# Router products in halves, product and sum as separate steps, last tile by column halves, in the tail of an attention and feed-forward kernel

## The chip, the cores and the metric

One core of a Trainium2 chip runs the whole layer in one launch. The metric is the device time of that core in microseconds (us); lower is better. The kernel before took 857.85 us, the median of three runs (856.19, 857.85 and 858.23).

## What is computed

```python
# x: (8, 128, 512); 32 heads of width 128; E = 8 routing experts
x = x + xattn(_layernorm(x), ctx, mask, ...)       # cross attention, with its own residual inside
xf = _layernorm(x).reshape(-1, 512)
routing = softmax(xf @ gate_w.T)                   # (1024, 8)
in_scale = routing @ in_channel_scale              # (1024, 512)
out_scale = routing @ out_channel_scale            # (1024, 512)
out = xf * in_scale @ sign(weight).T * out_scale + bias
x = x + out                                        # float32 throughout
```

The change touches the last part alone, the feed-forward with its router, which is done for eight tiles of 128 tokens by 512 channels.

## The kernel before, in words

The order of all work is written out by hand. `schedule()` (L84 and on) returns one list of steps such as `("M", 3, 1)`, and each engine walks the same list and picks the steps it has a function for, in that order (the `walk` calls at the end of each engine's block). Nothing is reordered later: if an engine waits in one step, all its later steps wait too. Engines signal each other by semaphores.

Most of the time goes into projections and attention. Float32 products are made of three products of rounded parts (high by high, high by low, low by high: `three`, L1268 to L1273). The stretch that matters here is the tail, the last 52 us. Its steps are, for a tile `i` of 8 or a pair `p` of 4 (pair `p` holds tiles `2p` and `2p+1`):

- `OUT`: the last attention output products; DVE (VectorE) adds them to `acc`. `ST`, `LN2`, `ROOT`, `LS`: statistics of the layer norm.
- `NT`, `BI`: the normalised tile (ACT, the ScalarE, or DVE for tiles 4 and 6), and the bias added to `acc` by POOL (GpSimd), L758.
- `TX`: the tile transposed on PE (TensorE) and copied by ACT.
- `G`: the router's logits for a pair, 8 products with 8 columns (L1390; the trace shows 16 matmuls), all written to the bank `t`; then the maxima on DVE (L1194) and the exponentials on ACT (L940).
- `ROUTE`: the division on DVE (L1202, L1205, L1209). `RT`, `RTC`: the routing weights transposed on PE (L1399) and copied by ACT (L949).
- `R`: the input scales of a pair, four 256-column products (L1410). `Y`: DVE multiplies them into the tiles (L1221, twice). `YL`: ACT makes the high part (L958, twice), DVE the low part of the first two channel chunks (L1229), POOL that of the other two (L771).
- `OS`: the output scale of one tile on PE (L1417), always into the one bank `out1`, and ACT's copy of it (L963). The next `OS` has to wait for that copy.
- `M`: the large product of a tile, eight 512-column matmuls in two parts of four (L1428, L1429), into bank `proj0` or `proj1` by turns.
- `MP`: three things of one tile in one step: DVE multiplies the product by the output scale (L1237), POOL adds it to `acc` (L779), SP (SyncE) stores the tile (L696). For the last tile DVE makes the sum itself (L1242).
- `KEEP`: six 512-column matmuls into `s1` that nothing reads (L1439).

The tiles of the product, `res_tiles`, are two buffers, so `MP` of tile `i` waits for POOL's sum of tile `i-2`. The large product of tile `i` waits for DVE's `MP` of tile `i-2`, which frees its bank.

## Time and profile before

| | |
|---|---|
| median of 3 runs | 857.85 us |
| the profiled execution, its own time | 855.55 us |
| its span, first to last instruction | 853.8 us |
| mean granted TensorE clock | 0.996 of full |
| PE, busy share of the span | 98% |
| tail, 800 to 854 us: PE, DVE, ACT, POOL busy | 46.2, 27.7, 24.9, 23.8 us |

The profile is one execution. Times of rows are counted from the start of its span. A busy PE is not PE at its peak: what matters here are the gaps between its matmuls and the clock that was granted. A gap is shown with the instruction that ended it.

### The profile page before, as it was taken

To read this page: it belongs to the slowest core of one execution; us is meant where nothing else is said; L and a number is where in the kernel's file an instruction comes from. 1 tells how busy PE (TensorE), PEld (TensorE's weight loads), DVE (VectorE), ACT (ScalarE), POOL (GpSimd) and SP (SyncE) were. 2 spreads that over 40 slices of the span, in tenths; PEclk is the share of its full clock that TensorE was granted. 3 is DMA by queue.
4 is the path that set the end of the run, shared out by engine and by line. 5 is a ranking of instruction groups with operands and counts; after the bars stand their busy time and mean duration, and the time that the engine had idled before them with its cause. 6 is when DMAs were issued, how large, how long until landed. Compare 5 with 4: busy or idle time off the path is not lost.

```text
span 853.8 us, 12843 instructions
## 1 busy us (share of the span) xinstructions
PE 840.0 (98%) x4354; PEld 703.1 (82%) x4354; DVE 623.4 (73%) x1000; ACT 391.8 (46%) x1007; POOL 302.9 (35%) x280
## 2 busy tenths in 40 slices
PE   9999999999999999999999999999999999999996
PEld 8878888888888877888888888888888888888874
DVE  5787846778776786868777777777777787787654
ACT  5632422432431444544544554454455445446662
POOL 2013211022030043525545544554454345434236
PEclk9999999999999999999999999999999999999999
DMA  8355463673443659414214313421441342150001
GB/s 272 134 178 181 157 226 135 183 256 133 133 166 111 222 190 292 143 53 152 99 59 152 135 53 125 152 104 55 154 141 54 116 152 99 59 210 8 1 25 74
DMA packets 60576, 114.07 MB, mean 134 GB/s; under 512 B 5192, under 2 KB 38600, under 8 KB 55264
## 3 DMA queue, kind: packets, MB, share of 16 engines
q1 hardware_dynamic: 60512, 113.25, 38.9%
q8 instruction: 36, 0.59, 0.3%
q14 instruction: 28, 0.23, 0.1%
HBM read 77.58 MB, written 35.65 MB: 133 GB/s over the span
## 4 chain that ended last, share of the span: by engine, by line
PE 87%; DVE 7%; ACT 2%; issue 2%; DMA 1%; POOL 0%; DVEq 0%; POOLq 0%; ACTq 0%; SPq 0%
PE out L1270 10%; PE out L1272 10%; PE out L1271 10%; PE proj L1270 9%; PE proj L1272 9%; PE proj L1271 9%; PE s L1342 6%; PE o L1361 6%; PE s L1272 3%; PE s L1270 3%; PE s L1271 3%; PE t L1350 3%; PE proj L1428 1%; PE proj L1429 1%; PE s L1318 1%
## 5 line engine op out<-in xcount | busy, mean ns | idle before, releaser
L878 ACT ACTIVATE probs<-probs,neg_max 128x128 f32<-128x128 f32 x256 | 99.7, 391 | 136.5 <-DVE neg_max L1132 136.4
L717 POOL TENSOR_TENSOR w_stage<-w_stage 128x256 f32<-128x256 f32 x30 | 24.5, 817 | 311.5 <-DMA w_stage<-in_wk 149.3
L729 POOL TENSOR_TENSOR w_lo<-w_stage,w_hi 128x512 fp32r<-128x512 f32 (+1 forms) x52 | 59.2, 1148 | 144.3 <-ACT w_hi L816 144.3
L1270 PE MATMUL out<-wo_hi,o_hi 128*128 128x512 f32 x224 | 95.3, 425 | 0.6 <-DVE acc L1166 0.6
L1166 DVE TENSOR_TENSOR acc<-out,acc 128x512 f32<-128x512 f32 x100 | 68.3, 687 | 34.4 <-PE out L1272 33.8
L1270 PE MATMUL proj<-x_hi,w_hi 128*128 128x512 f32 x210 | 88.5, 422 | 0.2 <-DVE ring L991 0.2
L1272 PE MATMUL out<-wo_lo,o_hi 128*128 128x512 f32 x224 | 88.3, 394 | 0.0
L1271 PE MATMUL out<-wo_hi,o_lo 128*128 128x512 f32 x224 | 87.6, 391 | 0.0
L1272 PE MATMUL proj<-x_lo,w_hi 128*128 128x512 f32 x210 | 82.7, 394 | 0.0
L1271 PE MATMUL proj<-x_hi,w_lo 128*128 128x512 f32 x210 | 82.0, 391 | 0.0
L741 POOL TENSOR_TENSOR bias_mask<-bias_raw,mask_neg 128x512 f32<-128x512 f32 x64 | 76.1, 1200 | 11.0 <-DVE probs L1129 10.9
L1139 DVE TENSOR_TENSOR probs<-probs,inv_sum 128x512 f32<-128x512 f32 x64 | 70.1, 1096 | 2.2
L816 ACT ACTIVATE w_hi<-w_stage 128x512 fp32r<-128x512 f32 (+1 forms) x113 | 61.7, 567 | 17.7 <-PE out L1272 3.4
L896 ACT ACTIVATE o_hi<-o 128x512 fp32r<-128x512 f32 x60 | 35.7, 595 | 46.7 <-PE o L1361 46.7
L1146 DVE TENSOR_TENSOR o_lo<-o,o_hi 128x512 fp32r<-128x512 f32 x60 | 41.0, 683 | 20.1 <-ACT o_hi L896 20.0
L1007 DVE TENSOR_TENSOR w_lo<-w_stage,w_hi 128x512 fp32r<-128x512 f32 (+1 forms) x61 | 42.8, 702 | 10.8 <-ACT w_hi L816 10.1
L1272 PEld LDWEIGHTS out<-wo_lo,o_hi 128*128 128x128 f32 x224 | 42.0, 188 | 9.5
L1270 PEld LDWEIGHTS out<-wo_hi,o_hi 128*128 128x128 f32 x224 | 42.3, 189 | 8.0 <-issue 2.1
L878 ACT ACTIVATION_READ_ACCUMULATOR probs<-probs,neg_max 128x1 f32 x256 | 47.9, 187 | 0.0
L1271 PEld LDWEIGHTS out<-wo_hi,o_lo 128*128 128x128 f32 x224 | 42.5, 190 | 6.0
L886 ACT ACTIVATE probs_t<-t 128x512 f32<-128x512 f32 x64 | 37.5, 586 | 21.1 <-PE t L1350 19.7
L1272 PEld LDWEIGHTS proj<-x_lo,w_hi 128*128 128x128 f32 x210 | 39.4, 188 | 9.0
(343 smaller groups left out, 2151.0 us busy)
## 6 DMA issues: line engine op xcount, KB each, us to landing
k_spill<-ring SPq DMA_DIRECT2D x64, 256.0 KB, 2.8
v_spill<-ring SPq DMA_DIRECT2D x64, 256.0 KB, 2.2
w_stage<-in_wk SPq DMA_DIRECT2D x32, 256.0 KB, 3.3
big_stage<-in_wv SPq DMA_DIRECT2D x8, 1024.0 KB, 7.9
w_stage<-in_wq SPq DMA_DIRECT2D x32, 256.0 KB, 4.2
k_first<-k_spill SPq DMA_DIRECT2D x8, 1024.0 KB, 6.6
v_first<-v_spill SPq DMA_DIRECT2D x8, 1024.0 KB, 4.8
wo_raw<-in_wo SPq DMA_DIRECT2D x16, 512.0 KB, 3.3
```

The lines of the kernel that those rows point to most:

```text
L729: pool.tensor_tensor(lo, staged(m, part), hi.bitcast(F32), ALU.subtract).then_inc(g_wlo, 1)
L741: pool.tensor_tensor(bias_mask[:, j % 2], bias_raw[:, i % 2][:, None, :].to_broadcast([P, HALF, P]), mask_neg[:, halves[half], :], ALU.add ...
L816: act.activation(hi, staged(m, part), ACT.Copy).then_inc(a_whi, 1)
L878: last = act.activation(probs[:, j % 2, b, :], probs[:, j % 2, b, :], ACT.Exp, bias=neg_max[:, col:col + 1], accum_out=row_sum[:, col:col ...
L1007: dve.tensor_tensor(lo, staged(m, part), hi.bitcast(F32), ALU.subtract).then_inc(v_wlo, 1)
L1139: dve.tensor_tensor(probs[:, j % 2], probs[:, j % 2], inv_sum[:, cols, None].to_broadcast([P, HALF, P]), ALU.mult).then_inc(v_probs, 1)
L1166: dve.tensor_tensor(acc[:, b, :], bank_tensor[:], acc[:, b, :], ALU.add).then_inc(v_acc, 1)
L1270: pe.matmul(to[:], left_hi, right_hi, start=first and n == 0, stop=False, skip_group_check=True)
L1271: pe.matmul(to[:], left_lo, right_hi, start=False, stop=False, skip_group_check=True)
L1272: last = pe.matmul(to[:], left_hi, right_lo, start=False, stop=n == len(pairs) - 1, skip_group_check=True)
L1342: last = pe.matmul(to[:, b * P:(b + 1) * P], queries[:, b * P:(b + 1) * P], keys, start=True, stop=True)
L1361: last = pe.matmul(to[:, b * P:(b + 1) * P], v_tiles[p % 2][:, half * HALF + b, i * P:(i + 1) * P], probs_t[:, j % 2, b * P:(b + 1) * P], ...
```

## The change

It is confined to the tail's order and to its last two tiles.

- The router's step is split: `GA` (first tile of a pair) and `G` (second tile), each 4 products, with other PE work between them for pairs 1, 2 and 3. DVE's and ACT's part stays at `G`.
- `MP` is split: `MP` is now DVE's product, and the new step `SUM` is the sum and the store. The sum of tile 6 goes from POOL to DVE.
- The last tile's large product is made by column halves: eight 256-column matmuls into `proj1`, then eight into `t`. DVE multiplies and adds each half by itself, and SP stores each by itself.
- `KEEP` is gone. The steps of the tail stand in another order.

```diff
+    def routed(p):
+        return [("RT", p), ("RTC", p)]
-              ("TX", 4), ("TX", 5), ("TX", 6), ("TX", 7), ("MP", 1), ("M", 2, 0), ("G", 2), ("ROUTE", 2), ("BI", 4), ("M", 2, 1), ("OS", 2),
-              ("M", 3, 0), ("RT", 2), ("RTC", 2), ("G", 3), ("R", 2), ("Y", 2), ("M", 3, 1), ("YL", 2), ("MP", 2), ("OS", 3), ("KEEP", 0),
-              ("OS", 4), *large(4), ("ROUTE", 3), ("RT", 3), ("RTC", 3), ("R", 3), ("Y", 3), ("MP", 3), ("BI", 5), ("OS", 5), *large(5),
-              ("YL", 3), ("MP", 4), ("BI", 6), ("OS", 6), *large(6), ("MP", 5), ("BI", 7), ("OS", 7), *large(7), ("MP", 6), ("MP", 7)]
...
+    steps += [("GA", 2), ("M", 2, 0), ("G", 2), ("BI", 4), ("M", 2, 1), ("ROUTE", 2), ("OS", 2), ("M", 3, 0), *routed(2), ("GA", 3),
+              ("R", 2), ("Y", 2), ("M", 3, 1), ("YL", 2), ("G", 3), ("MP", 2), ("SUM", 2), ("OS", 3), ("OS", 4), ("ROUTE", 3), ("BI", 5)]
+    steps += [("M", 4, 0), *routed(3), ("MP", 3), ("M", 4, 1), ("R", 3), ("Y", 3), ("YL", 3), ("SUM", 3), ("OS", 5), *large(5), ("MP", 4), ("BI", 6),
+              ("SUM", 4), ("OS", 6), *large(6), ("MP", 5), ("BI", 7), ("SUM", 5), ("OS", 7), *large(7), ("MP", 6), ("SUM", 6), ("MP", 7), ("SUM", 7)]
...
+                elif i == B - 1:
+                    dve.wait_ge(a_os, B)
+                    dve.wait_ge(g_res, B - 2)
                     dve.wait_ge(g_xb, B)
+                    for part, cols in enumerate(last_columns):
+                        dve.wait_ge(pe_ffn, B + part)
+                        dve.tensor_tensor(res_tiles[:, i % 2, cols], last_bank[part][:, 0:D // 2],
+                                          out_scale_halves[1][:, i % HALF, cols], ALU.mult).then_inc(v_prod, 1)
+                        dve.wait_ge(v_prod, B + part)
+                        dve.tensor_tensor(acc[:, i, cols], acc[:, i, cols], res_tiles[:, i % 2, cols], ALU.add).then_inc(v_last_res, 1)
...
-            def router(p):
-                if p == 0:
+            def router(p, r):
+                if p == 0 and r == 0:
                     pe.wait_ge(d_ffn_small, 80)
-                to = take(t_bank)
-                for i in (2 * p, 2 * p + 1):
-                    pe.wait_ge(a_nt, i + 1)
-                    for c in range(DC):
-                        last = pe.matmul(to[:, i % 2 * E:i % 2 * E + E], nt_pairs[p][:, i % 2, c * P:(c + 1) * P], gate_sb[:, c, :],
-                                         start=c == 0, stop=c == DC - 1)
...
-            def keep_busy(_):
-
-                to = take(s_bank[1])
-                for _ in range(KEEP_BUSY):
-                    last = pe.matmul(to[:], sign_w[:, 0, 0:P], sign_w[:, 0, :], start=True, stop=True)
-                last.then_inc(pe_kept, 1)
+            def last_product(part, toks):
+
+                to = take(last_bank[part])
+                for c in range(DC):
+                    pe.matmul(to[:, 0:D // 2], scaled_hi[:, c, toks], sign_w[:, c, last_columns[part]], start=c == 0, stop=False)
+                    last = pe.matmul(to[:, 0:D // 2], scaled_lo[:, c, toks], sign_w[:, c, last_columns[part]], start=False,
+                                     stop=c == DC - 1)
+                last.then_inc(pe_ffn, 1)
```

PE from the second part of tile 3 to the input scales of pair 3, before (L1417 is `OS`, L1439 `KEEP`, L1428 and L1429 a large product, L1399 `RT`, L1410 `R`):

```order
L1417 MATMUL out<-x_lo,x_hi 128x512
L1439 MATMUL s<-x_hi 128x512 x6
L1417 MATMUL out<-x_lo,x_hi 128x512
...
L1399 MATMUL s<-ident,routing 64x128 x2
L1410 MATMUL o<-x_hi,x_lo 128x256 x2
L1410 MATMUL out<-x_hi,x_lo 128x256 x2
```

and with the change (L1415 is the second half of the router for pair 3, L1449 `OS`, L1463 and L1464 a large product, L1431 `RT`, L1442 `R`):

```order
L1415 MATMUL t<-gate_sb,k_second 128x8 x4
L1449 MATMUL out<-x_lo,x_hi 128x512 x2
L1463 MATMUL proj<-x_hi 128x512
...
L1431 MATMUL s<-ident,routing 64x128 x2
L1463 MATMUL proj<-x_hi 128x512
...
L1442 MATMUL o<-x_hi,x_lo 128x256 x2
```

The six filling matmuls are gone, the router's second half stands directly ahead of two `OS` with nothing between them, and half of tile 4's large product has moved between `RT` and `R`.

DVE from the scaled tiles of pair 3 to its end, before (L1221 `Y`, L1237 `MP`, L1229 the low part of `YL`, L1242 the last sum):

```order
L1221 TENSOR_TENSOR k_second<-out0,k_second 128x512
L1237 TENSOR_TENSOR k_first<-proj1,v_first 128x512
L1229 TENSOR_TENSOR x_lo<-k_second,x_hi 128x2x256
L1237 TENSOR_TENSOR k_first<-proj0,v_second 128x512
L1237 TENSOR_TENSOR k_first<-proj1,v_second 128x512
L1237 TENSOR_TENSOR k_first<-proj0,v_second 128x512
L1237 TENSOR_TENSOR k_first<-proj1,v_second 128x512
L1242 TENSOR_TENSOR acc<-acc,k_first 128x512
```

and with the change (L1250 `MP`, L1232 `Y`, L1240 low part, L1258 the sum of tile 6, L1265 and L1268 product and sum of the last tile's halves):

```order
L1250 TENSOR_TENSOR k_first<-proj1,v_first 128x512
L1232 TENSOR_TENSOR k_second<-o,k_second 128x512
L1232 TENSOR_TENSOR k_second<-out0,k_second 128x512
L1240 TENSOR_TENSOR x_lo<-k_second,x_hi 128x2x256
...
L1250 TENSOR_TENSOR k_first<-proj0,v_second 128x512
L1258 TENSOR_TENSOR acc<-acc,k_first 128x512
L1265 TENSOR_TENSOR k_first<-proj1,v_second 128x256
L1268 TENSOR_TENSOR acc<-acc,k_first 128x256
L1265 TENSOR_TENSOR k_first<-t,v_second 128x256
L1268 TENSOR_TENSOR acc<-acc,k_first 128x256
```

`MP` of tile 3 moved ahead of `Y` of pair 3, and one sum of the old last tile became a sum of tile 6 and four half-width operations.

POOL's last operations, before (L779 a sum, L758 the bias, L771 its half of `YL`):

```order
L771 TENSOR_TENSOR x_lo<-wo_raw,x_hi 128x2x256
L779 TENSOR_TENSOR acc<-acc,k_first 128x512 x2
L758 TENSOR_TENSOR acc<-acc,ffn_bias_bc 128x512
L771 TENSOR_TENSOR x_lo<-k_second,x_hi 128x2x256
L779 TENSOR_TENSOR acc<-acc,k_first 128x512
```

and with the change (L790 a sum, L769 the bias, L782 its half of `YL`):

```order
L782 TENSOR_TENSOR x_lo<-wo_raw,x_hi 128x2x256
L790 TENSOR_TENSOR acc<-acc,k_first 128x512
L769 TENSOR_TENSOR acc<-acc,ffn_bias_bc 128x512
L782 TENSOR_TENSOR x_lo<-k_second,x_hi 128x2x256
L790 TENSOR_TENSOR acc<-acc,k_first 128x512
```

The sum of tile 3 moved from ahead of POOL's half of pair 3 to behind it; behind the rows shown stand a bias, a sum, a bias and a sum in both orders (tiles 6, 5, 7, 6 before; 6, 4, 7, 5 now).

## Rows read from the trace of the kernel before

**Rows 1.** The page: span, PE, and granted clock in 40 slices.
```profile
span 853.8 us, 12843 instructions
...
PEclk9999999999999999999999999999999999999999
```

**Rows 2.** Busy time by stretches (us: length, then each engine, clock, DMA share, GB/s).
```profile
800.00:854.00 54.00, 46.16 (x230) 34.84 (x228) 27.70 (x63) 24.86 (x53) 23.79 (x19) 0.94 0.11 40
```

**Rows 3.** The same view around the two slow stretches.
```profile
812.80:816.30 3.50, 3.50 (x11) 2.66 (x10) 2.69 (x11) 1.89 (x5) 1.40 (x1) 0.53 0.00 0
...
840.20:843.60 3.40, 3.31 (x8) 2.46 (x8) 1.23 (x3) 0.24 (x1) 3.29 (x3) 0.52 0.20 76
```

**Rows 4.** PE in order of time: start, us, what, [idle before, releaser].
```profile
802.15 0.48 PE L1270 MATMUL out<-x_lo,o_hi 128*128 128x512 f32 x1
...
808.17 0.38 PE L1399 MATMUL s<-ident,routing 128*64 128x128 f32 x2 [0.34 <-ACT w_stage L935]
...
810.54 1.95 PE L1390 MATMUL t<-gate_sb,w_stage 128*128 128x8 f32 x16
...
822.66 1.12 PE L1324 MATMUL s<-ident,ring 128*128 128x128 f32 x8 [0.34 <-ACT k_first L935]
...
837.81 0.50 PE L1410 MATMUL o<-x_hi,x_lo 64*128 64x256 f32 x2 [0.47 <-ACT x_hi L949]
838.15 0.39 PE L1410 MATMUL out<-x_hi,x_lo 64*128 64x256 f32 x2
838.38 0.39 PE L1417 MATMUL out<-x_lo,x_hi 64*128 64x512 f32 x1
840.29 0.78 PE L1428 MATMUL proj<-x_hi 128*128 128x512 f32 x1 [1.51 <-DVE k_first L1237]
```

**Rows 5.** The chain that ended last: start, us, what.
```profile
833.07 1.58 PE s L1439 x6
...
843.20 0.43 PE proj L1428
...
848.20 0.23 PE proj L1429
```

**Rows 6.** ACT in order of time.
```profile
831.10 0.27 ACT L940 ACTIVATE exps<-t,logit_neg_max 128x8 f32<-128x8 f32 x1 [1.52 <-DVE logit_neg_max L1194]
...
831.50 0.20 ACT L940 ACTIVATION_READ_ACCUMULATOR exps<-t,logit_neg_max 128x1 f32 x1
...
833.18 0.58 ACT L963 ACTIVATE v_first<-out 128x512 f32<-128x512 f32 x1
...
839.30 1.14 ACT L958 ACTIVATE x_hi<-k_second 128x512 fp32r<-128x512 f32 x2
```

**Rows 7.** DVE in order of time.
```profile
827.47 0.37 DVE L1205 TENSOR_SCALAR routing<-exps,exps_inv 128x16 fp32r<-128x16 f32 x2
...
834.19 1.74 DVE L1205 TENSOR_SCALAR routing<-exps,exps_inv 128x16 fp32r<-128x16 f32 x2
...
849.64 1.54 DVE L1242 TENSOR_TENSOR acc<-acc,k_first 128x512 f32<-128x512 f32 x1
```

**Rows 8.** POOL in order of time.
```profile
833.35 1.30 POOL L771 TENSOR_TENSOR x_lo<-wo_raw,x_hi 128x512 fp32r<-128x512 f32 x1 [7.18 <-ACT x_hi L958]
834.62 1.28 POOL L779 TENSOR_TENSOR acc<-acc,k_first 128x512 f32<-128x512 f32 x1
840.31 1.66 POOL L779 TENSOR_TENSOR acc<-acc,k_first 128x512 f32<-128x512 f32 x1 [4.42 <-DVE k_first L1237]
...
843.16 1.27 POOL L771 TENSOR_TENSOR x_lo<-k_second,x_hi 128x512 fp32r<-128x512 f32 x1
...
849.37 1.26 POOL L779 TENSOR_TENSOR acc<-acc,k_first 128x512 f32<-128x512 f32 x1
```

**Rows 9.** DVE's narrow tensor operation, from the groups by shape.
```profile
L1032 DVE TENSOR_TENSOR w_lo<-w_stage,w_hi 128x256 fp32r<-128x256 f32 x7 | 2.7, 421 | 4.3 <-ACT w_hi L832 4.3
```

**Rows 10.** The stores of the output, by tile: DMA time from issue to landing.
```profile
DMA to landing us min/median/max: 2.0/2.0/3.1
```

More of the change, by code:

```diff
@@ L691, in store @@
             def store(i):
-                if i < B - 1:
+                if i == B - 1:
+                    for part, cols in enumerate(last_columns):
+                        sp.wait_ge(v_last_res, part + 2)
+                        sp.dma_start(out[i][:, cols], acc[:, i, cols]).then_inc(d_out, 16)
+                    return
+                if i == B - 2:
+                    sp.wait_ge(v_last_res, 1)
+                else:
                     sp.wait_ge(g_res, i + 1)
-                else:
-                    sp.wait_ge(v_last_res, 1)
                 sp.dma_start(out[i], acc[:, i, :]).then_inc(d_out, 16)
             walk({"WL": pair_weights, "DL": second_plain_pair, "VL": value_weights, "SAVE": save, "ML": mask_load, "XL": x_load, "KV": keys_and_values,
-                  "BL": bias_load, "WOL": output_weights, "AL": residual_load, "SMALL": small_loads, "FW": ffn_weights, "MP": store})
-            sp.wait_ge(d_out, 16 * B)
+                  "BL": bias_load, "WOL": output_weights, "AL": residual_load, "SMALL": small_loads, "FW": ffn_weights, "SUM": store})
+            sp.wait_ge(d_out, 16 * (B + 1))
         @block.gpsimd
@@ L1381, in ffn_transpose, with first_router, second_router @@
                 read_by(ffn_bank(i), a_nt, i + 1)
-            def router(p):
-                if p == 0:
+            def router(p, r):
+                if p == 0 and r == 0:
                     pe.wait_ge(d_ffn_small, 80)
-                to = take(t_bank)
-                for i in (2 * p, 2 * p + 1):
-                    pe.wait_ge(a_nt, i + 1)
-                    for c in range(DC):
-                        last = pe.matmul(to[:, i % 2 * E:i % 2 * E + E], nt_pairs[p][:, i % 2, c * P:(c + 1) * P], gate_sb[:, c, :],
-                                         start=c == 0, stop=c == DC - 1)
-                last.then_inc(pe_gate, 1)
-                read_by(to, a_rexp, p + 1)
+                to = t_bank if r else take(t_bank)
+                pe.wait_ge(a_nt, 2 * p + r + 1)
+                for c in range(DC):
+                    last = pe.matmul(to[:, r * E:(r + 1) * E], nt_pairs[p][:, r, c * P:(c + 1) * P], gate_sb[:, c, :],
+                                     start=c == 0, stop=c == DC - 1)
+                if r:
+                    last.then_inc(pe_gate, 1)
+                    read_by(to, a_rexp, p + 1)
+            def first_router(p):
+                router(p, 0)
+            def second_router(p):
+                router(p, 1)
             def transpose_routing(p):
@@ L1433, in ffn_product @@
                     read_by(to, v_prod, i + 1)
[L1435 to L1440 removed]
+            def last_product(part, toks):
+                to = take(last_bank[part])
+                for c in range(DC):
+                    pe.matmul(to[:, 0:D // 2], scaled_hi[:, c, toks], sign_w[:, c, last_columns[part]], start=c == 0, stop=False)
+                    last = pe.matmul(to[:, 0:D // 2], scaled_lo[:, c, toks], sign_w[:, c, last_columns[part]], start=False,
+                                     stop=c == DC - 1)
+                last.then_inc(pe_ffn, 1)
             walk({"WARM": warm_up, "D": plain_product, "P": product, "X": transpose_x, "S": score, "T": transpose_probs,
[L1443 to L1444 removed]
+                  "PV": probs_times_values, "OUT": output, "TX": ffn_transpose, "GA": first_router, "G": second_router, "RT": transpose_routing,
+                  "R": routed_scales, "OS": routed_out_scale, "M": ffn_product})
 def kernel(**inputs):
```

37 lines of the change are left out of this document (22 added, 15 removed).

## The prediction, on record before the run

> **What bounds the kernel now.** I read the page first. PE is the busiest engine, and its clock is full in every one of the 40 slices [rows 1]. The change leaves everything up to about 802 us alone, so I read the tail by stretches: there the mean granted clock is 0.94 and PE is busy 46.2 of 54 us [rows 2]. At most some 8 us are thus in question. Smaller windows show the clock at 0.53 from 812.8 to 816.3 and at 0.52 from 840.2 to 843.6 [rows 3], which is its lower level, 1.2 GHz, nearly throughout. I call each a fall. The chain prices it: a large matmul takes 0.43 us at the low level and 0.23 at the full one [rows 5], so the eight in such a stretch lose 8 x 0.20 = 1.6 us. What PE did before each fall: 16 router matmuls with 8 columns in 1.95 us before the first; short products and waits of 0.47 and 1.51 us before the second [rows 4].
>
> PE's order of time shows its waits: 0.34 (`RT`, pair 0), 0.34 (`TX`), 0.47 (`R`, pair 3), 1.51 (large product of tile 5, behind DVE's `MP` of tile 3) [rows 4]. The chain shows the six filling matmuls in a row, 1.58 us [rows 5].
>
> The end is not PE's alone. POOL works without a break from 840.31 to 850.63, and DVE's last sum, 1.54 us against 0.6 to 0.7 for such an operation elsewhere, ends with POOL's last one plus about 0.55 us [rows 7, 8]. The same holding shows at 834.19: two small operations of DVE take 1.74 us while POOL runs two of its own, and 0.37 us where POOL is idle [rows 7, 8]. So there are two queues to follow: PE up to `R` of pair 3 (837.81), and from there PE beside POOL.
>
> **The change, step 1: from 802.15 to `R` of pair 3** (35.7 us before [rows 4]).
> - Filling matmuls: they stand on PE's path, -1.58 [rows 5].
> - Waits that go: the two of 0.34, and the 0.47, since half a large product (4 x 0.23 = 0.9) now lies between `RT` and `R`. -1.15 [rows 4].
> - The router in halves: the columns are the same, but PE starts slower after each change of kind; the first of 256 columns takes 0.34 for two where the next two take 0.23 [rows 4]. Some four to six more changes at 0.1: +0.4. The ends are 0.2 and 0.8.
> - New wait at `OS` 4. `OS` 3 and 4 stand together in one bank, and ACT must copy `OS` 3 between them. `G` 3 now comes just ahead, so ACT does its four exponential instructions first: maxima 0.2, exponentials 0.59 (831.10 to 831.70), copy 0.58 [rows 6]. That is 1.4, less the 0.33 that `OS` 3 itself takes: +1.1. Ends: 0.6 (if the copy starts at once) and 1.4.
> - New wait at `RT` 3. `ROUTE` 3 on DVE now follows `MP` 2, while POOL does its half of `YL` 2, the sum of tile 2 and now also the bias of tile 5 without a pause, 3 x 1.28 [rows 8]. DVE is held as in the 1.74 us row [rows 7], perhaps once more by the bias. Only half of tile 4's product covers it (0.9), where before there were `KEEP`, an `OS` and all of tile 4. I take +1.3. Ends: 0.3 (held once) and 1.4 + 1.2 = 2.6.
> - New waits in pair 2: `ROUTE` 2 meets POOL's sums of tiles 0 and 1 in the same way, +0.7 (0 to 1.3); tile 2's product follows the router's first half, before its bank is free, +0.5 (0 to 1).
> - Tiles 0 and 1 and pair 0: DVE has the same work in another order, 0.
>
> Sum: -1.58 - 1.15 + 0.4 + 1.1 + 1.3 + 0.7 + 0.5 = +1.27; I take **+1.2**. `R` of pair 3 starts at 839.0, later than before although the filling is gone.
>
> **Step 2: from `R` of pair 3 to the end** (853.8 - 837.81 = 16.0 before).
> - `Y`, then ACT's high parts: ended 840.44 before, 2.63 after `R` [rows 4, 6]. POOL's half of `YL` 3 began only at 843.16, because the sum of tile 3 and the bias of tile 5 stood ahead [rows 8]. Now neither does: it begins at 2.63.
> - POOL then has six operations, as before: 843.16 to 850.63 = 7.47 [rows 8].
> - DVE's last tile waits for the sum of tile 5, POOL's last. Then two half-width products and two half-width sums: 0.42 each [rows 9], 1.7 in all. With no POOL behind it nothing holds DVE.
> - From DVE's end to the span's end: 853.8 - 851.18 = 2.6 before. The last store is half as large. The nearest rows are the whole tiles, 2.0 to 3.1 from issue to landing [rows 10]; a half lies between the same and 0.3 less. I take 2.5.
>
> Together 2.63 + 7.47 + 1.7 + 2.5 = 14.3, which is **-1.7**.
>
> PE in step 2: from `R`, 0.57 to `OS` 5 [rows 4], three tiles at 0.4 + 8 x 0.23 = 2.3 with small waits, 0.5: ends 8.0 after `R`. The 16 half-width matmuls of the last tile cost what the eight full ones did: 0.23 for two [rows 4]. POOL ends 10.1 after `R`. So PE has 2 us to spare, the 1.51 us wait is gone without any gain of its own, and a fall there costs nothing.
>
> The sum of tile 6 is now DVE's and leaves POOL's queue. The Trainium skill ("GPSIMD Engine Reference", Key points) says that POOL shares its SBUF interfaces with VectorE and contends with DVE instructions that have two SBUF inputs. This sum is one. By that rule it is held by POOL's operations, as the last sum was (1.54 us in the trace, which agrees); it would start in POOL's last ones and be over before DVE's last tile may begin, so the sum above stands by either.
>
> **Sum against the profiled execution:** +1.2 - 1.7 = -0.5, with its two falls, the first on the path: 855.05 against 855.55.
>
> **Step 3: the clock.** The profiled execution is 2.3 us under the median of 857.85. Nothing else in the profile varies at this size, so I read the difference as 1.4 falls more on the path (2.3 / 1.6); this is inferred. Candidates are the router blocks, 1.8 us of almost no columns each. Three of four are now cut by large products, against which stand the new waits of 1.1 and 1.3 us and the missing filling. And late falls now cost nothing. I take 0.6 falls fewer on the path, -1.0. Ends: 2 fewer (-3.2) and 3 more (+4.8).
>
> The Trainium skill ("TensorE: Matmul & The Clock Gate", HAM oscillation) has a rule that speaks against this change: waits between groups of matmuls let the clock be throttled again, so PE should be kept busy. The trace agrees in kind, since the second fall follows waits; but the first follows no wait, only thin matmuls, and the filling did not prevent the second. The rule alone gives the third rival below.
>
> Against the median: -0.5 - 1.0 = -1.5, so **856.3 us**. A measurement of this kernel can tell about 0.3%, 2.6 us, from no change.
>
> **The rivals.**
> 1. *POOL's queue and held DVE eat the gain* (the forecast): 856.3. For it: POOL's unbroken row to 850.63. Chance 0.52.
> 2. *The waits do not come.* If `ROUTE` is not held and ACT copies in time, step 1 is -1.58 - 1.15 + 0.4 = -2.3 and all of step 2 follows it: -2.3 - 1.7 - 1.0 = -5.0 at most, 852.9; with half of the new waits, -3.2, 854.6. For it: POOL's hold on DVE shows in only two rows of the tail. Against: the `OS` wait is in the order itself. Chance 0.24.
> 3. *The clock falls more often*, the other side. With the filling gone, the stretch from `G` 3 to `R` 3 has waits of 1.1 and 1.3, half a router and an `OS` pair. Decides: when three falls more than before lie on the path (this one and two around the router's halves of pairs 1 and 2, whose new waits are 0.5 to 0.7). -0.5 + 3 x 1.6 = +4.3, 862.1; with two, +2.7, 860.5. For it: the first fall needed no wait at all. Against: large products lie between all halves. Chance 0.08.
> 4. *No fewer falls*: the order changes and the clock behaves as before, -0.5, 857.3. Chance 0.16.
>
> **How the numbers follow.** The forecast is the likeliest case. Faster by over 0.3% (under 855.3) is rival 2 with most of its values: 0.24. Slower by over 0.3% (over 860.4) is rival 3: 0.08. Within: 0.68. The range is to leave out the far half of rival 2 and most of rival 3, and the spread of the runs (2 us) lies in it: 853.8 to 859.2.
>
> **What would show it.** Right: `R` of pair 3 at 838 to 840; a wait of about 1 us at the second `OS` behind `G` 3; a wait at `RT` 3, with DVE's small `ROUTE` operations over 1 us long; POOL's half of `YL` 3 right after ACT and then POOL unbroken to the sum of tile 5; DVE's four half-width operations directly behind it; PE done some 2 us before POOL. Wrong: `R` of pair 3 before 837 (rival 2), windows at the low level at more than two places before it (rival 3), DVE's last product waiting for PE, or a store tail of over 3 us.

## The result and the profile after

Each line gives the median over the runs of a kernel and of the kernel before beside it, on the same chip.

| | changed | before | ratio (95%) |
|---|---|---|---|
| first | 853.23 (6 runs) | 856.12 (6) | 0.9963 (0.9948 to 0.9979) |
| again | 853.39 (12) | 855.38 (23) | 0.9976 (0.9962 to 0.9991) |
| profiled execution | 852.58, span 850.8 | 855.55, span 853.8 | |

The change is a gain of 2.0 to 2.9 us, 0.24% to 0.37%, where 1.5 us were forecast. The predicted time, 856.3, is 3.1 us too high, and 853.2 lies 0.6 us under the range. 2.4 us of the miss are the base: all 97 runs of the kernel before that stand beside the runs below have a median of 855.49, so 857.85 was 2.4 us high, and the profiled execution, 855.55, was an ordinary one.

The page of the kernel after, against [rows 1]:

```profile
span 850.8 us, 12849 instructions
...
PEclk9999999999999999999999999999999999999997
```

The stretches of the tail, against [rows 2, 3] (length, busy time and instructions of PE, PEld, DVE, ACT and POOL, granted clock, DMA share, GB/s):

```profile
800.00:851.00 51.00, 43.73 (x221) 33.08 (x219) 30.34 (x65) 23.96 (x52) 20.03 (x16) 0.89 0.12 42
...
812.80:816.30 3.50, 2.69 (x13) 1.95 (x14) 2.85 (x13) 1.87 (x3) 0.00 (x0) 1.00 0.00 0
833.40:843.20 9.80, 9.32 (x23) 6.14 (x24) 4.30 (x8) 2.69 (x5) 4.45 (x5) 0.50 0.14 50
```

The early low stretch is gone in this execution, and the late one is three times as long. The clock was thus lower over the tail than before, and the kernel still faster.

PE around the places of the prediction, against [rows 4]. The bracket is the idle time before and what ended it:

```profile
813.61 0.41 PE L1431 MATMUL s<-ident,routing 128*64 128x128 f32 x2 [1.08 <-DVE routing L1220]
...
821.33 0.50 PE L1463 MATMUL proj<-x_hi 128*128 128x512 f32 x1 [0.33 <-DVE k_first L1250]
...
826.18 0.41 PE L1431 MATMUL s<-ident,routing 128*64 128x128 f32 x2 [0.28 <-DVE routing L1220]
...
831.36 0.50 PE L1449 MATMUL out<-x_lo,x_hi 64*128 64x512 f32 x1 [0.97 <-ACT v_first L974]
...
833.88 0.63 PE L1431 MATMUL s<-ident,routing 128*64 128x128 f32 x2 [0.89 <-DVE routing L1220]
834.17 0.78 PE L1463 MATMUL proj<-x_hi 128*128 128x512 f32 x1
...
836.15 0.80 PE L1442 MATMUL o<-x_hi,x_lo 64*128 64x256 f32 x2
```

The waits forecast at `OS` 4 and `RT` 3 are there (0.97 and 0.89), and those of 0.47 ahead of `R` and 1.51 ahead of tile 5's product are not.

DVE, against [rows 7]:

```profile
831.05 1.41 DVE L1216 TENSOR_SCALAR routing<-exps,exps_inv 128x16 fp32r<-128x16 f32 x2
832.50 1.32 DVE L1220 SCALAR_TENSOR_TENSOR routing<-exps,exps_inv,routing 128x8 f32<-128x8 f32 x2
833.75 0.68 DVE L1250 TENSOR_TENSOR k_first<-proj,v_first 128x512 f32<-128x512 f32 x1
...
845.51 1.52 DVE L1258 TENSOR_TENSOR acc<-acc,k_first 128x512 f32<-128x512 f32 x1
846.95 0.41 DVE L1265 TENSOR_TENSOR k_first<-proj,v_second 128x256 f32<-128x256 f32 x1
847.40 0.42 DVE L1268 TENSOR_TENSOR acc<-acc,k_first 128x256 f32<-128x256 f32 x1
847.74 0.42 DVE L1265 TENSOR_TENSOR k_first<-t,v_second 128x256 f32<-128x256 f32 x1
848.19 0.43 DVE L1268 TENSOR_TENSOR acc<-acc,k_first 128x256 f32<-128x256 f32 x1
```

The small operations of `ROUTE` 3 are held twice, and the product of tile 3 (833.75) now stands ahead of `Y`. POOL, against [rows 8]:

```profile
832.39 1.27 POOL L769 TENSOR_TENSOR acc<-acc,ffn_bias_bc 128x512 f32<-128x512 f32 x1
839.01 1.28 POOL L782 TENSOR_TENSOR x_lo<-k_second,x_hi 128x512 fp32r<-128x512 f32 x1 [5.35 <-ACT x_hi L969]
840.25 1.27 POOL L790 TENSOR_TENSOR acc<-acc,k_first 128x512 f32<-128x512 f32 x1
...
845.19 1.29 POOL L790 TENSOR_TENSOR acc<-acc,k_first 128x512 f32<-128x512 f32 x1
```

POOL's half of `YL` 3 begins 2.86 us after `R` (839.01 - 836.15), where before it took 5.35 (843.16 - 837.81), and POOL is busy from there to 846.48. The chain that ended last runs along this:

```profile
845.23 1.26 POOL acc L790
846.49 0.04 DVEq L1264
846.53 0.43 issue
846.95 0.42 DVE k_first L1265
```

### The profile page after: what moved, and what is told of

Read it like the earlier page. It is cut to its first block, busy times and chain, and to the rows that moved or that the text cites. A ratio compares the mean times of both kernels' runs of the same rounds, so it can differ in the third digit from the quotient of the medians.

```text
span 850.8 us, 12849 instructions
## 1 busy us (share of the span) xinstructions
PE 837.7 (98%) x4356; PEld 703.6 (83%) x4356; DVE 622.6 (73%) x1003; ACT 390.9 (46%) x1007; POOL 302.8 (36%) x279
## 4 chain that ended last, share of the span: by engine, by line
PE 83%; DVE 7%; issue 4%; POOL 2%; ACT 2%; DMA 1%; POOLq 0%; DVEq 0%; ACTq 0%; SPq 0%
PE out L1296 10%; PE out L1298 10%; PE out L1297 10%; PE proj L1296 8%; PE proj L1298 8%; PE proj L1297 8%; PE o L1387 6%; PE s L1368 6%; PE s L1298 3%; PE s L1297 3%; PE s L1296 3%; PE t L1376 3%; PE s L1344 1%; POOL acc L790 1%; DMA w_stage<-in_wq 1%
## 5 line engine op out<-in xcount | busy, mean ns | idle before, releaser
L728 POOL TENSOR_TENSOR w_stage<-w_stage 128x256 f32<-128x256 f32 x30 | 26.6, 886 | 311.8 <-DMA w_stage<-in_wk 150.4
L1150 DVE TENSOR_TENSOR probs<-probs,inv_sum 128x512 f32<-128x512 f32 x64 | 67.9, 1061 | 2.2
```

The lines of the kernel that those rows point to most:

```text
L1150: dve.tensor_tensor(probs[:, j % 2], probs[:, j % 2], inv_sum[:, cols, None].to_broadcast([P, HALF, P]), ALU.mult).then_inc(v_probs, 1)
```

## The experiments

I take `TX` 0, PE's first transposes near 800 us, as the start of the tail. It lies between 798.9 and 802.3 in the 20 profiles, whatever was edited behind it. Of the 3.0 us between the first two profiles, 1.9 lie ahead of it (801.36 and 799.45). I take them for chance: over all profiles the mean start is 800.9 in the 6 built on the kernel before and 800.4 in the 14 built on the changed one, with a scatter of 3.4 in all. So I read each profile in two parts, `TX` 0 to `R` of pair 3, and `R` to the end of the span. Low clock is given in us at the lower level in the tail, up to PE's last matmul: the number of steps of 0.5 us with a granted clock under 0.95. "Low clock in a run" is an estimate, worked out from the mean clock c of a run of time T as T (1 - c) / 0.5; its mean over the runs of a kernel stands in the last column, in brackets.

| kernel | time (runs) | ratio to before (95%) | `TX` 0 to `R` | `R` to end | low clock, us (in a run) |
|---|---|---|---|---|---|
| before | 855.49 (97) | 1 | 36.45 | 15.99 | 7.5 (7.9) |
| before, second profile | 857.91 (1) | | 37.91 | 15.93 | 11.5 |
| changed | 853.23 (6) | 0.9963 (0.9948 to 0.9979) | 36.70 | 14.65 | 10.5 (8.5) |
| changed, second profile | 854.69 (1) | | 36.75 | 14.67 | 7 |
| changed, again | 853.39 (12) | 0.9976 (0.9962 to 0.9991) | 37.72 | 14.57 | 14.5 (10.1) |
| e1 filling back | 853.05 (5) | 0.9968 (0.9956 to 0.9981) | 36.65 | 14.45 | 4 (4.4) |
| e2 before, no filling | 855.97 (11) | 1.0005 (0.9994 to 1.0016) | 37.18 | 16.00 | 12 (14.2) |
| e3 old end | 853.94 (11) | 0.9976 (0.9962 to 0.9990) | 36.77 | 14.70 | 10.5 (9.5) |
| e4 new end alone | 856.18 (11) | 1.0007 (0.9998 to 1.0016) | 37.12 | 16.06 | 7.5 (7.3) |
| e5 biases early | 850.79 (6) | 0.9944 (0.9926 to 0.9961) | 36.30 | 13.38 | 10.5 (5.4) |
| e6 no holds | 849.44 (6) | 0.9932 (0.9912 to 0.9952) | 33.86 | 11.93 | 0 (3.4) |
| e6 again | 849.83 (6) | 0.9940 (0.9922 to 0.9958) | 35.24 | 12.07 | 3.5 (5.4) |
| e7 sum 3 ahead | 853.65 (12) | 0.9974 (0.9961 to 0.9988) | 36.75 | 13.45 | 7 (10.0) |
| e8 before, product 3 ahead | 852.64 (12) | 0.9963 (0.9949 to 0.9977) | 35.67 | 13.38 | 0 (4.4) |
| e9 routers whole | 857.74 (12) | 1.0020 (1.0001 to 1.0038) | 37.67 | 14.76 | 10.5 (15.5) |
| e9 again | 854.04 (1) | | 37.38 | 14.46 | 3.5 |
| e9, third | 855.17 (1) | | 37.71 | 14.73 | 10.5 |
| e9, fourth | 855.39 (1) | | 38.79 | 14.40 | 7.5 |
| e10 before, router halves | 856.84 (12) | 1.0010 (0.9997 to 1.0023) | 37.19 | 15.97 | 3.5 (6.7) |
| e11 product 3 back | 855.28 (12) | 1.0003 (0.9987 to 1.0019) | 36.13 | 15.92 | 7.5 (11.1) |

### The two kernels once more

Unchanged kernels, for the scatter of one profile and of the runs.

> The kernel before once more, unchanged, one look. Theory 2 (chance in the stretch before the tail): its first transposes of the tail start anywhere between 799 and 802 us. Rival: at 801.4 again, within 0.2 us.

> The changed kernel once more, unchanged, one look. Theory 2: its first transposes of the tail start anywhere between 799 and 802 us. Rival: at 799.5 again, within 0.2 us. Where the clock falls should differ from the first profile; from the first transposes to the end 51 to 53 us either way.

> The changed kernel again, timed beside the others. Theory 2 (the first six runs were a fair draw, the three runs of the kernel before shown first were not): 852.9 to 853.9, ratio to the kernel before 0.997 to 0.998. Rival (0.9963 is its true ratio): 852.4. The profile should show TensorE's low clock behind 828 us only.

The second part repeats within 0.1 us for each kernel: 15.99 and 15.93 before, 14.65, 14.67 and 14.57 changed. Its 1.3 us are therefore the change's. The first part scatters by 1.5 us before (36.45, 37.91) and by 1.0 changed (36.70, 36.75, 37.72); the means, 37.2 and 37.1, show no difference. The tail began at 802.26 and 801.48 in the second profiles, not where it did in the first (801.36 and 799.45), as the theory of chance has it. Where the clock falls moves too: in the second profile of before the low stretches lie at 813 to 817, 833.5 to 837 and 843.5 to 847.5, in the first at 813 and 840 only. The third profile of the changed kernel has a low stretch from 824.0 to 827.5, ahead of 828 us, where its forecast wanted none.

### The filling products

e1 puts them back into the changed kernel:

```diff
-... ("SUM", 2), ("OS", 3), ("OS", 4), ("ROUTE", 3), ("BI", 5)]
+... ("SUM", 2), ("OS", 3), ("KEEP", 0), ("OS", 4), ("ROUTE", 3), ("BI", 5)]
```

> The changed kernel with the six filling matmuls put back between OS 3 and OS 4 (1.58 us of PE time). Theory 1 (they filled a wait: OS 4 waits for ACT's copy, 0.97 us in the changed kernel's trace, and RT 3 waits for ROUTE 3 on DVE, 0.89 us, and POOL's chain sets the end): the start of R of pair 3, counted from the first transposes of the tail, moves by less than 0.3 us, and the time stays within 0.1% of the changed kernel. Rival (PE's path is what counts, as my prediction's first term has it): R starts 1.6 us later and the time rises by 1.6 us (+0.19%). Second rival (filling keeps the clock up): no low-clock stretch after 832 us in the profile, and the time falls by up to 1.6 us.

e2 takes them out of the kernel before:

```diff
-... ("MP", 2), ("OS", 3), ("KEEP", 0),
+... ("MP", 2), ("OS", 3),
```

> The kernel before without its six filling matmuls, nothing else. Theory 1: a wait of about 1.1 us at OS 4 and 0.3 to 0.4 us more at RT 3 take their place, R of pair 3 starts at the same distance from the tail's start within 0.3 us, time within 0.1% of the kernel before. Rival (the 1.58 us lie on the path): ratio 0.998. Rival (clock): one more low-clock stretch before R of pair 3, +1.6 us, ratio 1.002.

Neither moves the time by more than the scatter: 0.9968 with the filling beside 0.9963 and 0.9976 without it, and 1.0005 for e2. PE of e1 in order of time shows what the filling stands on:

```profile
831.97 2.85 PE L1484 MATMUL s<-x_hi 128*128 128x512 f32 x6
834.75 0.50 PE L1450 MATMUL out<-x_lo,x_hi 64*128 64x512 f32 x1
...
836.21 0.38 PE L1432 MATMUL s<-ident,routing 128*64 128x128 f32 x2
```

There is no wait at `OS` 4 or `RT` 3: the six matmuls fill both (this block fell into low clock, so it took 2.85 and not 1.58 us). PE of e2, without them, waits at `OS` 4 for ACT's copy of `OS` 3:

```profile
832.47 0.79 PE L1417 MATMUL out<-x_lo,x_hi 64*128 64x512 f32 x1 [0.74 <-ACT v_first L963]
```

So of the 1.58 us, 0.74 were the cover of a wait in the old order too. That leaves 0.84 for PE to gain, and e2 does not show it in its time. The clocks of the runs show where it went: without the filling e2 has 14.2 us of low clock in a run against 7.9 for the kernel before (a difference of 6.3 with a standard error of 0.8), and with it e1 has 4.4 against 9.6 for the changed kernel (5.1, standard error 1.4). So the filling does hold the clock up, by 5 to 6 us of low clock in a run, in both orders. In the old order e2's 6.3 us at 0.28 us each are some 1.8 us, more than the 0.84 that PE could gain; in the new order 5.1 us at 0.12 are 0.6. Both are estimates from the slopes given below. The rival of more low clock in e2 is thus right in kind, though its ratio of 1.002 isn't reached.

### The new end

e3 gives the changed kernel the old end (sum of tile 6 on POOL, the last tile whole, one store); e4 gives the new end to the kernel before.

```diff
-                if i >= B - 2:
+                if i == B - 1:
                     return
...
-                if i == B - 1:
-                    return
...
-                    for part, cols in enumerate(last_columns):
-                        dve.wait_ge(pe_ffn, B + part)
```

(e3 cut; e4 is the reverse, made in the kernel before.)

> The changed kernel with the old end: last product in one piece, the sum of tile 6 on POOL again, the last sum whole. Theory 1 (POOL's queue of six operations and then DVE's last tile set the end either way): the last sum ends about 0.55 us after POOL's last sum, POOL has one more operation (1.25 us) at its end, against DVE's four half-width ones (1.7 us) in the changed kernel; the time differs by 0.2 us, under 0.1%. Rival (the column halves and the moved sum are where the gain comes from): 1.5 us or more slower than the changed kernel.

> The kernel before with the new end alone: last product by column halves, tile 6's sum on DVE, four half-width operations of DVE, two half stores. Theory 1: 0.2 us faster than the kernel before, ratio 0.9995 to 1.000. Rival (the end is the gain): 1.5 us or more faster, ratio 0.998 or less. In all four runs the first transposes of the tail give the length of the untouched stretch before it: theory 2 (1.9 us of the 3.0 us between the two profiles are chance in that stretch) expects it to scatter over 1 to 2 us among these four profiles with no tie to the edit; its rival (something in the changed kernel shortens that stretch) expects 799.5 in the two built on the changed kernel and 801.4 in the two built on the kernel before.

0.9976 for e3 beside 0.9976 and 0.9963, and 1.0007 for e4. The end by parts is worth 0 to 0.13% in the new order, inside the scatter (each interval reaches 0.14% either way), and nothing can be seen of it in the old one. The tail began at 800.80, 800.02, 800.73 and 800.82 in e1 to e4, with no tie to the kernel that they were built on. DVE of e4 in order of time shows why:

```profile
847.25 1.61 DVE L1260 TENSOR_TENSOR acc<-acc,k_first 128x512 f32<-128x512 f32 x1
850.18 0.42 DVE L1246 TENSOR_TENSOR k_first<-proj,v_second 128x256 f32<-128x256 f32 x1 [1.32 <-POOL acc L765]
850.64 0.43 DVE L1249 TENSOR_TENSOR acc<-acc,k_first 128x256 f32<-128x256 f32 x1
850.98 0.42 DVE L1246 TENSOR_TENSOR k_first<-t,v_second 128x256 f32<-128x256 f32 x1
851.43 0.43 DVE L1249 TENSOR_TENSOR acc<-acc,k_first 128x256 f32<-128x256 f32 x1
```

The four half operations stand behind POOL's last one in a row of 1.7 us. Before, DVE's product was done by then and only the last sum was left, 0.55 us behind POOL [rows 7, 8]. What POOL is spared by handing over tile 6, the last tile pays back on DVE.

### POOL's queue: biases, sums and the holds

e5 moves the four biases of tiles 4 to 7 out of the tail's end (4 and 5 right behind their tiles, 6 and 7 behind `ROUTE` 2, with a wait of POOL for it):

```diff
-... ("NT", 7), ("OS", 0),
+... ("NT", 7), ("BI", 4), ("BI", 5), ("OS", 0),
...
-("G", 2), ("BI", 4), ("M", 2, 1), ("ROUTE", 2), ("OS", 2),
+("G", 2), ("M", 2, 1), ("ROUTE", 2), ("BI", 6), ("BI", 7), ("OS", 2),
```

> The changed kernel with POOL's bias additions moved ahead: tiles 4 and 5 right after their normalised tiles, 6 and 7 after ROUTE 2 (POOL waits for it). Same work. Theory 1 (POOL's queue sets the end and its operations hold DVE's ROUTE): between POOL's half of YL 3 and its last sum stand 4 operations instead of 6, 2.5 us less; ROUTE 2 and ROUTE 3 are held once less each. POOL then ends before PE, PE becomes the bound, and the time falls by 3 to 4 us, ratio to the kernel before 0.992 to 0.993. Rival (PE is the bound, the low clock above all): under 1 us faster than the changed kernel.

e6 is e5 with `OS` 3 ahead of `G` 3 and the sum of tile 2 behind `ROUTE` 3 (with a wait of POOL for it):

```diff
-("G", 3), ("MP", 2), ("SUM", 2), ("OS", 3), ("OS", 4), ("ROUTE", 3)]
+("OS", 3), ("G", 3), ("MP", 2), ("OS", 4), ("ROUTE", 3), ("SUM", 2)]
```

> As the one above, with OS 3 ahead of the second half of router 3, so that ACT's copy lies beside it, and POOL's sum of tile 2 behind ROUTE 3. Theory 1: the waits at OS 4 (0.97 us) and RT 3 (0.89 us) are gone or under 0.4 us, R of pair 3 starts 0.9 us earlier than in the one above, no low-clock stretch behind 830 us in most executions; time 4.5 to 6 us under the changed kernel, ratio to before 0.990 to 0.992. Rival (the waits only move on, to ROUTE 3's own chain): the same as the one above within 0.3 us.

> The version with POOL's biases early, OS 3 ahead of router 3's second half and the sum of tile 2 behind ROUTE 3, timed again. Theory 1: 849 to 850 us, ratio to before 0.992 to 0.994. Rival (the first six runs were lucky): over 851.

e5 gains 0.2% to 0.3% on the changed kernel, some 2.5 us where 3 to 4 were expected, and `R` to the end goes from 14.65 to 13.38: with two operations of 1.25 us fewer, POOL ends at 844.23 and PE (846.61), at the lower clock from 831 to 841.5, is the bound. It also splits the hold. In e5's order of time, DVE's first small group is held by POOL's sum of tile 2, and the second, which the bias of tile 5 held for 1.32 us, is free:

```profile
831.16 1.39 DVE L1218 TENSOR_SCALAR routing<-exps,exps_inv 128x16 fp32r<-128x16 f32 x2
832.59 0.36 DVE L1222 SCALAR_TENSOR_TENSOR routing<-exps,exps_inv,routing 128x8 f32<-128x8 f32 x2
```

In e6 both are free, the same operations on the same data:

```profile
832.67 0.37 DVE L1220 TENSOR_SCALAR routing<-exps,exps_inv 128x16 fp32r<-128x16 f32 x2
833.08 0.36 DVE L1224 SCALAR_TENSOR_TENSOR routing<-exps,exps_inv,routing 128x8 f32<-128x8 f32 x2
```

e6 is the fastest kernel of the study, 849.44 and 849.83 in its two timings, 3.4 to 4.0 us under the changed kernel (4.5 to 6 were expected) and some 6 under the kernel before. Most of it is e5's: e6 lies 1.0 to 1.4 us under e5, and their intervals overlap. In the two profiles e6 reaches `R` 1.1 and 2.4 us sooner than e5; that its second part is 1.3 to 1.5 us shorter goes at least in part with the clock, which was low for 5 us behind `R` in e5 and for none in the first profile of e6. POOL's row ends at 842.43, 0.9 ahead of PE (843.29). The chain that ended last still runs along POOL's three sums to 842.44 and, 0.46 us later, into DVE's four operations, as in the changed kernel. PE stands level with POOL here; it has not replaced it as the bound.

e7 puts the sum of tile 3 ahead of POOL's half of `YL` 3, into the gap of 5.35 us:

```diff
-("R", 3), ("Y", 3), ("YL", 3), ("SUM", 3), ("OS", 5),
+("R", 3), ("Y", 3), ("SUM", 3), ("YL", 3), ("OS", 5),
```

> The changed kernel with POOL's (and only POOL's and SP's) sum and store of tile 3 ahead of its half of YL 3, as the order before had it. POOL stands idle for 5.3 us ahead of YL 3, and the product of tile 3 is there long before. Theory 1 (what gained is that DVE's product of tile 3 comes ahead of Y 3, and POOL's queue behind YL 3 sets the end): POOL has 5 operations from YL 3 on instead of 6, its end comes 1.25 us earlier after R of pair 3, and the time falls by 0 to 1.2 us (less where a low clock makes PE as late). Rival (the move of the sum behind YL 3 is what gained): R of pair 3 to the end grows from 14.6 back towards 16.0 us, and the time rises by 1 us or more.

It takes 1.2 us off the second part of its profile (13.45), yet the median, 853.65, is that of the changed kernel. The intervals would hold a gain of about 1 us, hardly the whole 1.2. The profile says one thing and the timing another. I take the timing; why is open, and it counts against reading POOL's queue as the only bound of every run.

### Which step carries the gain

e8 makes one move in the kernel before, `MP` of tile 3 (product, sum and store) from behind `Y` to ahead of `RT`. e11 undoes the move in the changed kernel and restores the old order on POOL there.

```diff
e8:
-*large(4), ("ROUTE", 3), ("RT", 3), ("RTC", 3), ("R", 3), ("Y", 3), ("MP", 3), ("BI", 5),
+*large(4), ("ROUTE", 3), ("MP", 3), ("RT", 3), ("RTC", 3), ("R", 3), ("Y", 3), ("BI", 5),
e11:
-("OS", 4), ("ROUTE", 3), ("BI", 5)]
+("OS", 4), ("ROUTE", 3)]
-*routed(3), ("MP", 3), ("M", 4, 1), ("R", 3), ("Y", 3), ("YL", 3), ("SUM", 3), ("OS", 5),
+*routed(3), ("M", 4, 1), ("R", 3), ("Y", 3), ("MP", 3), ("SUM", 3), ("BI", 5), ("YL", 3), ("OS", 5),
```

> The kernel before with one step moved: MP of tile 3 ahead of RT 3, so that DVE multiplies tile 3 ahead of Y 3 and POOL's sum of tile 3 can start early. Theory 1: PE's wait of 1.51 us ahead of tile 5's product goes, POOL's half of YL 3 starts 2.6 us after R of pair 3 instead of 5.3, and R to the end is 13.3 to 14.0 us instead of 16.0; ratio to the kernel before 0.997, that is, as good as the whole change. Rival (the gain needs the whole order): R to the end stays over 15.5 us, ratio over 0.999.

> The changed kernel with tile 3's product on DVE behind Y 3 again, and POOL's sum of tile 3 and bias of tile 5 ahead of its half of YL 3, as in the order before; all else as changed. Theory 1 (that one move is the gain): PE waits 1.5 us for tile 5's product again, R of pair 3 to the end is back at 15.5 to 16.0 us instead of 14.6; R itself may come 1 us earlier, since the bias no longer holds ROUTE 3; the time rises by 0.5 to 1.5 us over the changed kernel. Rival (the halves, the end or the filling carry the gain): within 0.3 us of the changed kernel.

e8 alone reaches 0.9963, all that the change reaches, with the filling, the whole routers and the old end still there. e11 has everything but this move and is back at 1.0003. One thing more differs in e8: its runs had less low clock, 4.4 us in a run against 7.9 for the kernel before. At 0.28 us of time for a us of low clock (below) that is about 1 us of its gain of 2.8 to 3.2; the difference is clear of the scatter (3.4 with a standard error of 1.0), but how the move brings it is not shown. PE in order of time, e8 and then e11, at the same two places:

```profile
835.72 0.50 PE L1410 MATMUL o<-x_hi,x_lo 64*128 64x256 f32 x2 [0.47 <-ACT x_hi L949]
...
836.62 0.50 PE L1428 MATMUL proj<-x_hi 128*128 128x512 f32 x1
```

```profile
837.76 0.73 PE L1463 MATMUL proj<-x_hi 128*128 128x512 f32 x1 [1.51 <-DVE k_first L1250]
```

POOL in order of time, e8 and then e11:

```profile
834.90 1.26 POOL L779 TENSOR_TENSOR acc<-acc,k_first 128x512 f32<-128x512 f32 x1 [1.11 <-DVE k_first L1237]
...
838.45 1.28 POOL L771 TENSOR_TENSOR x_lo<-k_second,x_hi 128x512 fp32r<-128x512 f32 x1 [1.04 <-ACT x_hi L958]
...
844.67 1.25 POOL L779 TENSOR_TENSOR acc<-acc,k_first 128x512 f32<-128x512 f32 x1
```

```profile
837.78 1.66 POOL L790 TENSOR_TENSOR acc<-acc,k_first 128x512 f32<-128x512 f32 x1 [5.66 <-DVE k_first L1250]
...
840.64 1.28 POOL L782 TENSOR_TENSOR x_lo<-k_second,x_hi 128x512 fp32r<-128x512 f32 x1
```

In e8 POOL makes the sum and the bias while it would have waited for ACT, and its half of `YL` 3 begins 2.73 us after `R`. In e11 it begins 5.36 after `R` (835.28), as before. The move does two things at once: it brings POOL forward and it takes away PE's wait of 1.51 us. No run does one of them alone. In the kernel before the two engines bounded the end nearly together: the chain that ended last ran over DVE's product of tile 3, PE's matmuls behind it up to 848.89 and DVE's last product, and the bias of tile 7 that the last sum also needs left POOL at 849.40. Had POOL alone come forward, DVE's last sum could have begun at 849.6 as it did and, not held, taken 0.7 instead of 1.54 us. By this estimate from the rows that is a gain of about 0.8 us, where the second part is 1.3 us shorter in the changed kernel and 2.6 in e8.

### The routers in two parts

e9 puts each router of the changed kernel back in one piece, directly ahead of its second half; e10 splits them in the kernel before.

```diff
e9 (pair 2; 1 and 3 alike):
-("GA", 2), ("M", 2, 0), ("G", 2),
+("M", 2, 0), ("GA", 2), ("G", 2),
e10 (pair 2; 1 alike; of pair 3 the second half moves behind M 3, 1):
-("MP", 1), ("M", 2, 0), ("G", 2),
+("MP", 1), ("GA", 2), ("M", 2, 0), ("G", 2),
```

> The changed kernel with the router's two halves of each pair together again. Theory 3 (the halves keep the clock from falling around the router): a low-clock stretch around 811 to 816 us or 822 to 828 us comes back, as in three of the four profiles of kernels with whole routers and in none of the five with halves; time 1 to 1.6 us more than the changed kernel. Rival (where it falls is chance, or it is the other order that matters): no fall before 828 us, and the time within 0.5 us of the changed kernel.

> The kernel before with the router in halves (pairs 1 to 3) and nothing else. Theory 3: no low-clock stretch before 828 us; what it saves in falls it loses, since the second half of router 3 now comes later, ahead of OS 3, and ROUTE 3 with it: up to 2 us. The time is within 1 us of the kernel before. Rival (halving alone is the gain): 1.5 us or more faster. Rival (halving only costs): 2 us slower with the same falls as before.

> The changed kernel with whole routers again, one look, since its runs fall in two groups (854.6 to 855.7 and 857.3 to 860.5, with mean clocks of 0.994 to 0.997 and 0.986 to 0.993) and its profile was of the first. Theory 3: where the mean clock is 0.990 or less, the profile has low-clock stretches around the routers of pairs 0 to 2 (804 to 828 us), 12 us or more of low clock ahead of R of pair 3. Rival: the low clock lies behind 828 us there too, only longer.

> A third look at the changed kernel with whole routers, for its slow group (half of its timed runs). Theory 3: if the time is over 857 us, low-clock stretches lie between 804 and 828 us, around the routers of pairs 0 to 2. Rival: they lie behind 828 us only. If the time is under 856 us it says nothing new.

> A fourth look at the changed kernel with whole routers, with the same expectations as the third: over 857 us, theory 3 expects low clock between 804 and 828 us; under 856 us it says nothing new.

In the old order the halves bring nothing (1.0010, from 0.9997 to 1.0023). The profile of e10 has no low clock ahead of `R` and still needs 37.19 us to it, where e8, with whole routers, product 3 ahead and no low clock either, needs 35.67. This suggests that what the halves may save there in clock they cost in time, as the forecast of e10 had it. In the new order the median of whole routers lies 4.4 us over the changed kernel. The mean clock of e9's runs is 0.9910 against 0.9941 to 0.9950 for the changed kernel, about 15 us of low clock in a run against 8.5 to 10. The 12 times lie in two groups, five from 854.6 to 855.7 and seven from 857.3 to 860.5, so the median stands for neither: the lower group is 1 to 2.5 us over the changed kernel and the upper 4 to 7. The four profiled executions of this kernel took 855.25, 854.04, 855.17 and 855.39, so none belongs to the upper group. Three of them are single runs on two other chips, so how often the upper group comes up there isn't known. The windows of the first:

```profile
800.00:828.00 28.00, 25.91 (x153) 20.86 (x152) 16.84 (x44) 17.98 (x38) 10.34 (x9) 1.00 0.05 19
...
833.50:844.00 10.50, 10.11 (x25) 6.54 (x25) 5.96 (x10) 3.02 (x6) 4.81 (x4) 0.51 0.07 26
```

Here the low clock lies where the changed kernel's does, as in the second and third (from 834 and from 833.5). Only the fourth has a low stretch at the router of pair 2, 825.0 to 828.5, and the changed kernel, with halves, had one at the same place (824.0 to 827.5). So the theory that halves keep the clock from falling there isn't borne out by the profiles. What they do show is a first part of 37.9 us in the mean of four against 37.1 for the changed kernel. That the executions of the upper group have a further low stretch around a router block fits the clock, but it was not seen; where it lies stays open.

## Why the prediction was wrong

**Step 1, to `R` of pair 3: +1.2 forecast, +0.25 in the first pair of profiles, nothing in the means.** The new waits were forecast at 1.1 + 1.3 + 0.7 + 0.5 = 3.6. Measured in the first profile: `OS` 4 0.97, `RT` 3 0.89, `RT` 2 0.28, tile 2's product 0.33, together 2.47, and one of 1.08 at `RT` of pair 1 (813.61), for which the prediction has no term. The sum, 3.55, is right by luck. The mechanism at `RT` 3 is as stated: two small groups of 1.41 and 1.32 us instead of 0.37 and 0.36, the second held by the bias, as e5 shows by moving it. The Trainium skill ("GPSIMD Engine Reference", Key points) says that POOL shares its SBUF interfaces with VectorE and contends with operations that have two SBUF inputs or run in a 2-port mode. The trace agrees for the sum of tile 6, which has two SBUF inputs (1.52 us). The held operation of 128x16 has one tensor input and a scalar per partition; whether it ran in such a mode, no run here shows. With the measured waits the sum of step 1 stays at -1.58 - 1.15 + 0.4 + 3.55 = +1.2. Between it and the +0.25 lies the clock, which I had left to step 3: the low stretch at 813 is gone (-1.6), and a later one begins ahead of `R` (the four matmuls from 834.17 to 836.15 take 1.98 where 4 x 0.23 and a change of kind make 1.0: +1.0). That gives +0.6; the last 0.35 us I can't place. So the waits were sized rightly in sum and did not lengthen the stretch by what the sum says. The +0.4 for the router's halves was not measured by itself.

**Step 2, `R` to the end: -1.7 forecast, -1.34 measured, and the same in every repeat.** Term by term: POOL's half of `YL` 3 at 2.86 (forecast 2.63; `Y` ran behind matmuls at the lower clock), POOL's six operations 7.47 (7.47), DVE behind POOL 2.14 (1.7: the four operations take 1.7, and 0.47 pass between POOL's end and DVE's first start, the 0.04 and 0.43 of the chain above), store and end 2.2 (2.5). This is the part of the prediction that held, and e8 and e11 show that it carries the gain. PE ended 2.0 us ahead of POOL in the second profile (846.98, 848.98), as forecast. In the first it ended 0.8 behind (847.28, 846.48), since 7 of the 9.8 us of low clock lay behind `R`.

**The total came close by luck.** The forecast was +1.2 - 1.7 - 1.0 = -1.5, the last term for fewer low stretches. The two parts of the tail give -0.1 and -1.3 in the means of the profiles, -1.4: step 1 came out 1.3 lower than forecast, and this made up for the 1.0 of the clock, which did not come as fewer low stretches, and for 0.4 in step 2. The runs give -2.0 to -2.9. A part of the rest lies in the price of the low clock, as the next paragraph has it.

**Step 3 failed, in its first sentence.** The profiled execution was 2.3 us under the median of three runs, and I read this as 1.4 low stretches that the median had and the profile had not. The runs beside the experiments put the kernel at 855.49 (97 runs) with a standard deviation of 1.3 us; the three runs happened to be high and the profile was typical. Had I set the whole -1.5 against the profiled execution of 855.55, it would have given 854.05, 0.8 above the result; but its -1.0 rests on the same reading, and without it the sum gives 855.05, 1.8 above. That late low stretches cost less in the new order was right in kind. Over the runs, a us of low clock goes with 0.28 us of time in the kernel before (97 runs) and with 0.12 in the changed one (18 runs), each with a standard error of 0.04. The straight lines through these runs stand 1.3 us apart at no low clock (853.4 and 852.2) and 2.5 at eight us of it: the gain grows with the low clock that a run has. But the low clock did not become less: 8.5 and 10 us in a run against 7.9. The missing filling accounts for that and more, for with it back (e1) it is 4.4.

**The rivals.** *The waits do not come* did not happen: they came, in full. Its time, 852.9 to 854.6, is where the result lies, for another reason. *The clock falls more often* did not decide here, but it is not idle: e9, the same order without the halves, has the lower mean clock and the longer time, +4.4 us in the median. The 0.08 was then low for a kernel one edit away. The Trainium skill ("TensorE: Matmul & The Clock Gate", HAM oscillation) lays such losses to waits between groups of matmuls. The clocks agree: e1, which fills the waits, has 4.4 us of low clock in a run and the changed kernel, which has them, 9.6. In time it is worth little here, 853.05 against 853.23 and 853.39.

**What the parts are worth.** Product of tile 3 ahead of `Y`: the whole gain (e8, e11). Filling: nothing that shows in the time either way (e1, e2), since a good part of it only fills waits and the rest pays for itself by the clock. Parts of the last tile: 0 to 0.13%, inside the scatter (e3, e4). Halves of the routers: nothing in the old order, and in the new one they keep off a loss of 0.4% to 0.6% in the median (e9, e10). I priced all but the first with care and gave the first, as a "1.51 us wait [that] is gone without any gain of its own", a clause. Its worth was that POOL's sum and bias no longer stand ahead of its half of `YL` 3, by which POOL's row ends sooner. That the wait of PE had no gain of its own is not shown: as said at e8 and e11, POOL's gain would have stopped at some 0.8 us with PE where it was.

## What to carry to other kernels

When an engine works through its queue in order, look for the item that waits for late data while urgent work stands behind it. One product moved ahead of the scaled tiles gave all of this change's gain, by what it let POOL do early and by the wait that it took from PE. An operation of POOL beside VectorE has two prices, its own place in the queue and 0.9 to 1.4 us on a pair of small operations of VectorE that meets it, so place such operations where neither is on the path (e5 and e6 together: another 3.4 to 4.0 us, most of it by e5). Take the base of a comparison from many runs: three runs misled by 2.4 us, about what the change was worth (2.0 to 2.9).

## What the runs showed of the hardware

- POOL's hold takes in tiny operations of VectorE: two of 128x16 take 1.39 to 1.74 us beside POOL's 128x512 sums and 0.37 beside none (kernel before, changed kernel, e5, e6), two of 128x8 take 1.32 beside a 128x512 bias and 0.36 without it (changed kernel, e5).
- Where TensorE's clock falls differs between executions of one kernel (813 and 840 in one, 813, 833.5 and 843.5 in the next), and six filling matmuls made it rarer without ruling it out: 4.4 us of low clock in a run with them against 9.6 without in the new order, 7.9 against 14.2 in the old; in e1's profile a low stretch begins at 831, just ahead of them (831.97).
- Most low clock of the new order lies at 832 to 844, behind `OS` 3 and 4, `RT` 3 and `R` 3. It costs less there (0.12 us for a us of it, against 0.28 in the kernel before); in the profiles of the changed kernel the chain ends over POOL. With the biases and the holds out of the way, e6 had none in one profile (mean clock 1.00 from 800 us on) and 3.5 us in the other.
